# A recurrent layer's columns in time order instead of row order

## What is computed

```python
xn = layernorm(x, ln_w, ln_b)
u = xn @ Ws.T + bs + xn @ Wi.T + bi            # 16 values a token
h[t] = tanh(h[t-1] @ A.T + u[t])               # 256 steps, each needs the one before
out = h @ Wo.T + bo
gate = sigmoid(xn @ Wg.T + bg)
x = layernorm(x + out * gate + x)
x = layernorm(x + moe(x) + x)                  # softmax router, top 2 of 8, and a shared expert
```

## Time and profile before

| | us |
|---|---|
| median of 3 runs | 537.75 (537.72 to 538.87) |
| span of the profiled execution, first to last instruction | 536.5 |
| TensorE matmuls busy | 478.4 (89%) |
| TensorE weight loads busy | 381.2 (71%) |
| VectorE busy | 341.1 (64%) |
| ScalarE busy | 337.4 (63%) |
| GpSimd busy | 305.0 (57%) |

### The profile page before, as it was taken

One profiled execution on the slowest core, in us unless ns is written; L12 is line 12 of the kernel. 1 busy time (PEld: TensorE's weight loads), 2 busy tenths in 40 slices (PEclk: granted clock), 3 DMA queues, 4 the chain that ended last, 5 costly groups with the idle time before them and its releaser, 6 DMA issues.

```text
span 536.5 us, 11146 instructions
## 1 busy us (share of the span) xinstructions
PE 478.4 (89%) x2842; PEld 381.2 (71%) x2842; DVE 341.1 (64%) x1514; ACT 337.4 (63%) x870; POOL 305.0 (57%) x337
## 2 busy tenths in 40 slices
PE   5889999999999999897899857999999999999871
PEld 3657777777777777686788746988888888767530
DVE  5353579797979788746575763445454467667752
ACT  3654777777677776435567524677777777777553
POOL 4000003676766676467377777777657777885331
PEclk9977999999999999759999878899999999999987
DMA  3771112232233222278446476558657888841682
GB/s 107 151 235 56 49 47 63 88 92 87 90 90 91 89 72 74 67 220 231 122 140 188 130 215 202 156 140 246 200 167 214 228 264 270 250 167 62 225 288 78
DMA packets 58228, 79.81 MB, mean 149 GB/s; under 512 B 11182, under 2 KB 37803, under 8 KB 58166
## 3 DMA queue, kind: packets, MB, share of 16 engines
q1 hardware_dynamic: 48940, 61.64, 39.7%
q0 software_dynamic: 8640, 16.93, 9.3%
q10 hardware_dynamic: 586, 0.53, 0.3%
HBM read 47.85 MB, written 25.84 MB: 137 GB/s over the span
## 4 chain that ended last, share of the span: by engine, by line
PE 72%; DVE 10%; issue 5%; ACT 5%; DMA 3%; SPq 2%; ACTq 1%; POOL 1%; DVEq 0%; POOLq 0%
PE pu L1342 13%; PE py L1287 9%; PE p L1270 8%; PE py L1288 7%; PE p L1275 7%; PE ph L1280 7%; PE pt L1424 3%; PE pm L1401 3%; DMA weights<-ys 2%; PE pu L1229 2%; ACT hT L656 2%; PE pm L1358 2%; DVE z L1076 2%; PE pu L1380 1%; PE pu L1377 1%
## 5 line engine op out<-in xcount | busy, mean ns | idle before, releaser
L574 POOL DMA_INDIRECT ys<-yp,xp x142 | 141.4, 996 | 55.8 <-issue 38.4
L567 POOL DMA_INDIRECT xs<-x,place_i x128 | 124.1, 970 | 68.4 <-ACT hT L656 28.1
L656 ACT ACTIVATE hT<-pu,bu 16x32 f32<-16x32 f32 x256 | 78.6, 307 | 78.3 <-PE pu L1342 74.3
L1342 PEld LDWEIGHTS pu<-hT,aT 128*128 128x128 f32 x512 | 81.8, 200 | 58.2 <-ACT hT L656 52.8
L1342 PE MATMUL pu<-hT,aT 128*128 128x32 f32 x512 | 105.7, 293 | 11.6 <-ACT hT L656 11.5
L647 ACT ACTIVATE hid<-z 128x512 f32<-128x512 f32 x103 | 64.7, 628 | 65.3 <-DVE z L1076 63.3
L1071 DVE SCALAR_TENSOR_TENSOR z<-p,wp,t3a 128x256 f32<-128x256 f32 x71 | 34.3, 483 | 78.5 <-ACT t3a L635 68.0
L1287 PE MATMUL py<-wp,hid 128*128 128x128 f32 x284 | 60.4, 295 | 14.2 <-DVE yp L1097 12.0
L1287 PEld LDWEIGHTS py<-wp,hid 128*128 128x128 f32 x284 | 46.0, 196 | 29.8 <-DVE yp L1097 19.9
L555 POOL TENSOR_TENSOR rstd_in<-ve_in,neghalf 128x4 f32<-128x4 f32 x16 | 16.4, 1026 | 73.8 <-DVE ve_in L793 73.7
L1288 PE MATMUL py<-wp,hid 128*128 128x128 f32 x284 | 56.6, 282 | 0.0
(11 more groups left out here) (264 smaller groups left out, 984.4 us busy)
## 6 DMA issues: line engine op xcount, KB each, us to landing
wp<-packed SPq DMA_DIRECT2D x71, 320.0 KB, 3.3
xp<-xs SPq DMA_DIRECT2D x71, 130.0 KB, 2.9
weights<-ys SPq DMA_DIRECT2D x16, 512.0 KB, 4.4
xt<-in_L_attn_x SPq DMA_DIRECT2D x16, 256.0 KB, 3.1
x<-x SPq DMA_DIRECT2D x16, 256.0 KB, 2.7
packed<-weights SPq DMA_DIRECT2D x1, 2560.0 KB, 8.6
ys<-yp,xp POOLq DMA_INDIRECT x142, 3.0
yb<-x SPq DMA_DIRECT2D x16, 128.0 KB, 2.8
```

The source lines that it names most:

```text
L567: g.indirect_dma_start(out=xs[:, :], out_offset=bass.IndirectOffsetOnAxis(ap=place_i[b % NB][:, c, t * Q + q:t * Q + q + 1], axis=0), in_= ...
L574: g.indirect_dma_start(out=ys[:, :], out_offset=bass.IndirectOffsetOnAxis(ap=xp[j % NX][:, h, DEST:DEST + 1].bitcast(int32), axis=0), in_= ...
L656: nc.scalar.activation(hT[k % 2][0:N, c], pu[k % 2][0:N, c], ACT.Tanh, bias=bu[:, 0:1]).then_inc(h_ready, 1)
L1342: nc.tensor.matmul(pu[k % 2][:, step_cols(t)], aT[:, :], before, start=False, stop=True, skip_group_check=True).then_inc(h_ps, 1)
```

## The change

`step_cols` and two new views. In the four places where a tile's 512 columns cross between row order and time order or are used by a step, the addresses change; nothing else does. In row order column q*128 + 4 b + tq is batch b at step 4 tq + q, so a step's 32 columns lie four elements apart. In time order it is column 128 tq + 32 q + b, so they lie side by side, 16 steps one after the other. The crossing is done by the copy of the transposed input (L667), which reads pm with a stride of four elements and writes runs of 64, half of the rows at a time, and by the gated output (L1121), which reads gth and pu in order and writes og with a stride of four elements, back in row order.

```diff
         def step_cols(t):
             tq, q = divmod(t, Q)
-            return slice(q * P + tq, (q + 1) * P, STEPS // Q)
+            return slice(tq * P + q * B, tq * P + (q + 1) * B)
+
+        def by_step(bank, half=None):
+
+            cols = bank[:, :].rearrange("d (t r) -> d t r", r=P)
+            return cols if half is None else cols[:, :, half * P // 2:(half + 1) * P // 2]
+
+        def by_row(cols):
+
+            return cols.rearrange("d (r t) -> d t r", t=STEPS // Q)
...
-                        ins = nc.scalar.activation(xnT[k % 2][:, cols], pm[:, cols], ACT.Identity, scale=lnw, bias=lnb)
+                        ins = nc.scalar.activation(by_step(xnT[k % 2], h), by_row(pm[:, cols]), ACT.Identity, scale=lnw, bias=lnb)
...
-                    nc.vector.scalar_tensor_tensor(out=og[:, :], in0=gth[k % NG][:, :], scalar=1.0, in1=pu[k % 2][:, :],
+                    nc.vector.scalar_tensor_tensor(out=by_row(og[:, :]), in0=by_step(gth[k % NG]), scalar=1.0, in1=by_step(pu[k % 2]),
                                                    op0=ALU.add, op1=ALU.mult).then_inc(og_ready, 1)
```

## The result

| | before | changed |
|---|---|---|
| median of 4 runs, us | 538.31 (537.72 to 539.38) | 532.0 (528.38 to 535.61) |
| ratio | | 0.9894, 95% interval 0.9849 to 0.9939 |
| span of the profiled execution | 536.5 | 532.3 |
| that execution's own time | not given | 534.11 |
| last tanh starts | 250.6 | 244.3 |

The change is faster by 1.1%, 6.3 us between the medians; the forecast was 531.0, in a range of 526.0 to 538.5. A second series, beside other kernels, gave 532.19 against 536.93, 0.9863 (0.9803 to 0.9923). Single runs differ by 8 us, more than the gain, so I read the steps from the traces and use the medians only for signs.

A forecast was written before the change was run, and what follows sets the result against it. Alternating matmul and tanh turns of 0.82 us were taken to bound the recurrence. Tanh -8.3, xnT's copy +0.7 and og +0.8 gave -6.8 us: a span of 529.7 plus 1.25 around it, 531.0 us, range 526.0 to 538.5.

The forecast's parts named there:

- The turn between TensorE and ScalarE sets the recurrence: Recurrence: matmul and tanh alternate in turns of 0.82 us; 13.5 of a tile's 16 steps gain from a shorter turn.
- The tanh, 45 ns less: Each step's tanh, now on adjacent columns, drops 45 ns from 308; over the paying turns 8.3 us less.
- The step's matmul, 0: TensorE's matmul of a step gains nothing from adjacent columns; rounding of the starts leaves up to 20 ns.
- Rival (a): The step's matmul gains too, since non-contiguous PSUM access slows matmuls: 15 ns a turn, 2.8 us more gain, 528.2; chance 0.12.
- 185 turns: Turns that pay: 256 steps less tile 0's and the start's 21 and tile 15's 16, times 13.5/16.
- xnT's copy, +0.7 us: Copy of the transposed input, reading PSUM at 16 bytes, grows 50 ns; 14 tiles make 0.7 us more.
- Rival (c): The price sits in the PSUM read: xnT's copy grows 0.36 us, cancelling the tanh's gain; 537.5, no change; chance 0.10.
- og, +0.43 us and two tiles, 0.8 us: Gated output's spread write on VectorE takes 0.43 us longer, uncovered only in tiles 0 and 13: 0.8 us more.
- 0.70 us are free: Slack between tile 10's og and TensorE's loads, taken as the least of the other tiles, so og's 0.43 is covered.
- The sum, -6.8 us: Whole kernel: -8.3 for the tanh, +0.7 for xnT's copy, +0.8 for og.
- rival (b): Half of the gain is lost behind the recurrence, in GpSimd's queue or TensorE's clock: 3.4 us lost, 534.4; chance 0.12.
- Rival (d): Slower: a spread costs only in long streams; tanh stays 308 ns, xnT costs 3.0 us, og 0.8: 541.6; chance 0.14.

The follow-up runs named there:

- h_two_apart: Kernel before with a step's hT columns 8 bytes apart and og without crossing back; 641.67 us on another chip, where the kernel before took 659.92.
- og_write_alone: Kernel before with only og's write spread over 16 bytes an element, the crossing before og left out; 540.17 us, ratio 1.0002 (0.9966 to 1.0039).

## Why the prediction was right

- **The turn between TensorE and ScalarE sets the recurrence**: right. Every ordinary turn shortened by what its two instructions lost. The gate's step lost 0.03 us; of the two steps at the logits one stayed at 0.93 and one gained 0.04, so 13.5 turns a tile was right.
- **The tanh, 45 ns less**: right in kind, too large. It lost 30, next to the 32 that the row of the third's bias copy gave. I had chosen nearer to the gate's tanh because it was the same function, and had carried a slope of rows from SBUF over 224 columns: a slope off by 0.1 ns a column is 22 ns, as much as half of the term. Over the 13.5 turns of a tile the 38 ns measured give 0.51 us, and tile 7 took 0.50 less.
- **The step's matmul, 0**: nearly. 8 ns a turn went beside the tanh. The line through 8 and 128 columns gave 0.458 against 0.46, and starts rounded to 10 ns could not show it. Rival (a) thus had a small part of the truth, though not by PSUM's side, which it named.
- **185 turns**: tiles 0 to 2 gained nothing in this run (tile 3 starts at 60.0 us, 59.9 before), though I had counted 27 steps of tiles 1 and 2. Besides the wait in tile 0 there were one more step of 1.49 us at the low clock and a longer wait. On the other side tile 15, which I had not counted, took 25.9 us instead of 28.5, since the clock was at its low level (1.2 GHz) for 10 us there instead of 17. Tiles 0 to 2 vary between kernels whatever their layout, from 43.9 to 49.2 us. Tile 15 does not: the three traces with a tanh of 308 ns have 28.4 to 28.6 us there, 17 of them at the low clock, and the seven with 278, those on another chip (see h_two_apart) left aside, 25.6 to 27.2 with 10 to 14. So it goes with the shorter turn, by a way that no run here shows. Busy time over tile 15, before and changed (the granted clock is the last number but two, 0.70 and 0.80):

```profile
222.10:250.90 28.80, 24.44 (x126) 21.17 (x125) 16.26 (x72) 13.08 (x37) 17.20 (x20) 0.70 0.70 197
```

```profile
218.40:244.60 26.20, 21.90 (x126) 19.01 (x125) 16.46 (x70) 12.75 (x37) 16.13 (x19) 0.80 0.75 213
```

- **xnT's copy, +0.7 us**: 0, 543 ns in both. The row of a PSUM read with hops, 4 ns above the slope, had nearly said so. Rival (c) fell with it.
- **og, +0.43 us and two tiles, 0.8 us**: the size was right (0.40, and not the other estimate's 0.74). It costs for tile 13's og as forecast, and for two more, 1.3 us in the three and 1.5 in tiles 3 to 14. The step that failed is "0.70 us are free", twice over. It was not the least of the other tiles: tile 11's og ends at 184.83 in the kernel before, and its loads start at 185.18, 0.35 us.

```profile
184.15 0.68 DVE L1121 SCALAR_TENSOR_TENSOR og<-gth,pu 128x512 f32<-128x512 f32 x1
...
185.18 0.50 PEld L1229 LDWEIGHTS pu<-ident,og 128*128 128x128 f32 x4
```

  And slack was read at the old pace. Tile 10's fell from 0.70 to 0.12 with og still at 0.68 us, since, counted from the first tanh of the tile whose steps they stand in, og starts 0.46 us later than before (2.87 instead of 2.41) and its transposes 0.12 earlier (3.67 instead of 3.79); the prediction called the cover thin but did not subtract its own gain from it. And in one of the three places what waited was not og's reader but a copy behind og.
- **The sum, -6.8 us**: -6.3 between the medians and -6.3 at the last tanh, and that it came so near is in part luck. Of the 6.3 at the last tanh tiles 3 to 14, which hold 162 of the 185 turns, give 3.9 (158.36 us against 162.22), where the forecast's own terms give 6.3 for them (7.3 for the tanh, less 0.6 for xnT and 0.4 for og); tile 15, which the sum left out, gives 2.5, and tiles 0 to 2 take 0.1 back. What the tanh, sized half too large, and og, which cost nearly twice what was forecast, took from the sum, tile 15 made up for.
- **What is lost behind the recurrence**: in the profiled spans only -4.2 is left. Behind the last tanh the changed kernel took 288.0 and 287.1 us in its two traces, the kernel before 285.9, and the kernels without a spread og 283.1 to 286.6. og_write_alone, with og spread, took 284.2, which speaks against og as the cause, though its router saw other values. The cause stays open, and rival (b) stays open to about 2 us.
- **Rival (d)**, that a spread costs only in long streams, fell: 32 elements paid about 1 ns each, xnT's 256 nothing. What decides is the memory, not the length.

## What to carry to other kernels

Where a layout has to be crossed, let the crossing be a strided read from PSUM, and keep two fp32 elements in every 16 bytes of each SBUF access: here that took the addresses of three instructions (the tanh, the step's matmul, og) and left xnT's copy and gth alone. On a path where two engines take turns, tens of nanoseconds in one small instruction count hundreds of times, so compare it with the same instruction on adjacent addresses first. And read the slack of everything else at the new pace, not at the old one.

## What the runs showed of the hardware that I had not expected

- One fp32 element in 16 bytes of SBUF costs ScalarE's write 0.8 to 1 ns (304 and 308 against 277 ns for 32) and VectorE's write 0.78 ns (1079 against 680 for 512); two in 16 bytes, neighbours or not, cost ScalarE 2 ns in 279. VectorE's SBUF read with 512-byte hops costs 0.70 ns (1038 against 681), beside a PSUM input with the same hops.
- PSUM read by ScalarE at 16 bytes (xnT 543 and 543 ns) and at 512-byte hops (gth 448 and 449), and by VectorE at 512 (og 680), is free; so is TensorE's write at 16 bytes (147.6 us for 176 steps either way).
- The same kernel's single runs differ by up to 1.8% (533.7 to 543.1 us for the kernel before in one series), and the times broadly follow the mean granted clock: for the change, 526.9 us at 0.966 and 533.1 to 535.0 at 0.945 to 0.951. A gain of 1% in such a kernel is to be read in the trace.
